# A graph kernel whose adjacency is loaded by quarters of columns and turned by VectorE instead of TensorE

## The chip, the cores and the metric

The kernel runs on one core of one Trainium2 chip. The metric is the time on the device of one execution in microseconds; where there are several runs, their median is given.

## What is computed

Two graph layers over 4096 nodes with 256 features, each behind a layer norm and a ReLU, each added to its input:

```python
# layer 1
mask = (adj > 0)                                  # adj: 4096 x 4096 int32
agg  = mask @ h / max(rowsum(mask), 1)
out  = relu(concat(h @ W_self + b_self, agg @ W_nb + b_nb) @ W_comb + b_comb)
# layer 2, 4 heads of 64
Wh = h @ W ; sl, sr = Wh . a_l, Wh . a_r
e  = leaky_relu(sl[i] + sr[j]) where adj[i, j] + (i == j) > 0, else -inf
out = elu(softmax(e) @ Wh)
# both:  x = x + layer(relu(layernorm(x)))
```

The adjacency is 64 MB of int32, and is read once.

## The kernel before

The program is written out for each engine by hand, with semaphores between them; what stands in an engine's block is the order in which it works, and `Fori` loops run the steady parts.

**First phase (to about 76 us).** `x` comes in 16 pairs of rows (256 nodes each) by SP's queue. They are normed and multiplied with the folded weights; the result is `g`, 16-bit high and low parts of the neighbour product for all 4096 nodes, and `own`, the node's own part, stored to HBM by GpSimd's queue.

**First layer (32 tiles of 128 nodes).** For a tile t, SP's queue loads its rows of the adjacency in two halves of 2048 columns into `stage` (`adj_rows`, L319), each as soon as the half before it in the same buffer is unpacked. VectorE turns int32 into bytes of 0 or 0xB8, the fp8 code of a number (`to_bits`, L946). ScalarE sums the bytes into the degree (L718). TensorE takes two bytes as one bf16 and transposes 16 blocks of 128x128 (`words`, L553); VectorE copies them from PSUM to `mT` (`copy_words`, L957), and GpSimd keeps a second copy in `mask` for layer 2 (`keep`, L433). TensorE then sums `g` over the neighbours: 32 products, each with weights of fp8 bytes read from `mT` at a step of two bytes (`sums`, L567). `post` (L969 to L994) makes x1 of the tile from the sum, the degree and the rows that GpSimd's queue brings back (L441), and its norm's numbers; ScalarE writes the normed h1 (L728). TensorE turns h1 (L577) and multiplies it with W (L586). These two stand in the middle and at the end of the next tile's sums. `set_self_edges` (L1008) sets the diagonal in `mask`, once for two tiles.

**Second layer (from about 379 us).** For each of 4 heads and 4 strips of 1024 nodes: ScalarE and VectorE write signs as bytes (L778, L1044), VectorE combines them with `mask` (L1054, L1065), and TensorE sums values over bytes of both results (`branch`, L630), 8192 products of 130 columns. These too read fp8 weights at a step of two bytes.

Of the kernel before, what the change touches and what calls it, by code (L numbers as in the profile page):

```python
# [23 lines left out]
F32 = mybir.dt.float32  # L24
F16 = mybir.dt.float16
BF16 = mybir.dt.bfloat16
# [29 lines left out]
VBLK = 2 * DV  # L56
CH = 4
NCH = NK // CH
NQ = NK // 2
ZR = 8  # L60
PR = 4


def build(nc, x, adj, W_self, b_self, W_nb, b_nb, W_comb, b_comb, W, a_l, a_r, out):
# [8 lines left out]
    out_v = out.rearrange("(s k p e) (h d) -> s h e p k d", s=NS, p=P, e=2, h=H)  # L73
    x_v = x.rearrange("(k p e) d -> k p (e d)", p=P, e=2)
    adj_v = adj.rearrange("(k p e) m -> k p (e m)", p=P, e=2)
    HALF = N // 2
    HK = NK // 2
    NP2 = NK // 2
    E1 = D + 3 * H
    WS = STRIP // 2  # L80
    with ExitStack() as ctx:
# [15 lines left out]
        mask32 = mask[:, :, :].bitcast(I32)  # L97
        sr = sb("sr", [P, NT, 3 * H], F32)
        diag = sb("diag", [P, 2 * P], U16)
# [3 lines left out]
        identb = sb("identb", [P, P], BF16)  # L103
# [11 lines left out]
        diagf = early(5, 2 * D, 2 * P).rearrange("p (e n) -> p e n", e=2)  # L115
        bcol = early(5, 2 * D + 2 * P, 4)
# [9 lines left out]
        shift = early(13, 64, 2)  # L126

# [3 lines left out]
        degp = sb("degp", [P, NT, 2], F32)  # L131
        mT = sb("mT", [P, 2, N // 2], BF16)
# [3 lines left out]
        deg = sb("deg", [P, 3], F32)  # L136
# [10 lines left out]
        shift1 = sb("shift1", [P, 1], F32)  # L147
# [22 lines left out]
        pos = mT[:, :, :].rearrange("p e m -> p (e m)").bitcast(I32).rearrange("p (k n) -> p k n", k=PR)  # L170
# [13 lines left out]
        ps_t = [t.bitcast(BF16) for t in ps_t32]  # L184
# [32 lines left out]
        stage_in = [sem(f"stage_in{i}") for i in range(2)]  # L217
# [3 lines left out]
        words_ready = sem("words_ready")  # L221
        words_copied = sem("words_copied")
        kept = sem("kept")
# [7 lines left out]
        norm1_ready = sem("norm1_ready")  # L231
# [65 lines left out]
        def _(sp):  # L297
# [25 lines left out]
            adj_rows(0, 0)  # L323
# [6 lines left out]
            adj_rows(0, 1)  # L330
            with sp.Fori(1, NK) as k:
                for e in range(2):
                    adj_rows(k, e)
# [7 lines left out]
            sp.wait_ge(words_ready, NT * 2)  # L341
            sp.wait_ge(deg_ready, NT * 2)
# [28 lines left out]
            def store(gr):  # L371
                sp.wait_ge(y_ready, gr + 1)
                for e in range(2):
                    sp.dma_start(out_v[gr % NS, gr // NS, e],
                                 y[:, :, :].rearrange("p (k e) d -> p e k d", e=2)[:, e]).then_inc(stored, 16)

            def next_s(gr):

                sp.wait_ge(act_signs, gr * ASIGN)
                sp.wait_ge(dve_signs, gr * DSIGN)  # L380
                load_s(gr + 1)
# [18 lines left out]
            sp.wait_ge(stored, 32 * NG)  # L400

        @block.gpsimd
        def _(pool):
            nc.gpsimd.memset(ident[:, :], 0.0).then_inc(zeroed, 1)
            nc.gpsimd.memset(diagf, 0.0).then_inc(zeroed, 1)
            nc.gpsimd.memset(ones[:, :], 1.0)
            nc.gpsimd.memset(eps[:, :], EPS).then_inc(consts, 1)
            pool.wait_ge(zeroed, 2)
            nc.gpsimd.affine_select(out=ident[:, :], in_=ident[:, :], compare_op=ALU.not_equal, fill=1.0,
                                    base=0, pattern=[[-1, P]], channel_multiplier=1).then_inc(consts, 1)  # L410
            for e in range(2):
                nc.gpsimd.affine_select(out=diagf[:, e, :], in_=diagf[:, e, :], compare_op=ALU.not_equal,
                                        fill=float(ONE << (8 * e)), base=0, pattern=[[-1, P]],
                                        channel_multiplier=1).then_inc(consts, 1)
# [67 lines left out]
        def _(pe):  # L482
# [74 lines left out]
            def sums(t, e, f):  # L557
# [11 lines left out]
                if f == 1:  # L569
                    last.then_inc(agg_ready, 1)  # L570
# [720 lines left out]
```

## Time and profile before

| | us |
|---|---|
| median of 3 runs (889.4 to 891.55) | 890.43 |
| the profiled execution | 888.39 |
| its span, first to last instruction | 886.8 |

| engine | busy us | share of the span |
|---|---|---|
| TensorE, products | 824.4 | 93% |
| TensorE, weight loads (beside the products) | 659.3 | 74% |
| VectorE | 719.6 | 81% |
| ScalarE | 696.3 | 79% |
| GpSimd | 153.4 | 17% |

The share is an average over three stages. The DMA engines, whose mean share is given beside the engines, moved 115 MB, 67 MB of it adjacency, nearly all of it in the first layer. A row by form gives a line of the program, the engine, what it writes and reads, how often, and the mean time of one in ns.

### The profile page before, as it was taken

To read this page: it belongs to the slowest core of one execution; us is meant where nothing else is said; L and a number is where in the kernel's file an instruction comes from. 1 tells how busy PE (TensorE), PEld (TensorE's weight loads), DVE (VectorE), ACT (ScalarE), POOL (GpSimd) and SP (SyncE) were. 2 spreads that over 40 slices of the span, in tenths; PEclk is the share of its full clock that TensorE was granted. 3 is DMA by queue.
4 is the path that set the end of the run, shared out by engine and by line. 5 is a ranking of instruction groups with operands and counts; after the bars stand their busy time and mean duration, and the time that the engine had idled before them with its cause. 6 is when DMAs were issued, how large, how long until landed. Compare 5 with 4: busy or idle time off the path is not lost.

```text
span 886.8 us, 26720 instructions
## 1 busy us (share of the span) xinstructions
PE 824.4 (93%) x10276; PEld 659.3 (74%) x10276; DVE 719.6 (81%) x1373; ACT 696.3 (79%) x989; POOL 153.4 (17%) x221
## 2 busy tenths in 40 slices
PE   3998899999999999869899989999899999899996
PEld 3343355555555555449899989999899999899996
DVE  3897677787778777578879898888998889989885
ACT  2675556666666666488989999999998999989993
POOL 0111345454646463300000000000000000000000
PEclk9999899999999999969999999999999999999998
DMA  6345767878787878540041011121101410111011
GB/s 219 111 150 210 281 243 281 306 278 312 279 312 273 313 277 308 91 111 23 2 95 48 0 48 48 37 58 48 48 14 33 95 47 6 42 48 47 0 24 35
DMA packets 74875, 115.32 MB, mean 130 GB/s; under 512 B 55553, under 2 KB 57473, under 8 KB 66657
## 3 DMA queue, kind: packets, MB, share of 16 engines
q1 hardware_dynamic: 67472, 94.19, 32.2%
q0 software_dynamic: 7376, 20.85, 7.4%
q8 instruction: 8, 0.13, 0.1%
q14 instruction: 19, 0.15, 0.1%
HBM read 98.17 MB, written 16.85 MB: 130 GB/s over the span
## 4 chain that ended last, share of the span: by engine, by line
PE 66%; DVE 16%; ACT 7%; issue 5%; DMA 4%; DVEq 1%; SPq 1%; ACTq 0%
PE ps_a L567 12%; PE ps_t L630 12%; PE ps_x L630 12%; PE ps_a L630 11%; PE ps_h L630 6%; PE ps_w L630 6%; DMA stage<-in_adj 3%; ACT stage L778 3%; DVE bits L946 3%; DVE stage L1054 2%; PE ps_x L525 1%; PE ps_t L553 1%; PE ps_w L586 1%; PE ps_a L525 1%; ACT late L728 1%
## 5 line engine op out<-in xcount | busy, mean ns | idle before, releaser
L567 PE MATMUL ps_a<-g,mT 128*128 128x512 f16 x1024 | 234.8, 383 | 2.5 <-DVE mT L957 2.5
L778 ACT ACTIVATE stage<-bits,sr 128x1024 int8<-128x1024 f32 x192 | 203.6, 1167 | 1.1 <-PE ps_w L630 1.1
L778 ACT ACTIVATE stage<-rows,sr 128x1024 int8<-128x1024 f32 x192 | 203.1, 1172 | 1.1 <-PE ps_w L630 1.1
L1054 DVE SCALAR_TENSOR_TENSOR stage<-stage,mask 128x1024 int32<-128x1024 int32 x128 | 156.4, 1222 | 42.1 <-ACT stage L778 41.6
L567 PEld LDWEIGHTS ps_a<-g,mT 128*128 128x128 fp8e4 x1024 | 100.9, 99 | 112.7 <-issue 7.4
L718 ACT ACTIVATE junk<-bits 128x2048 uint8<-128x2048 uint8 x64 | 122.2, 1910 | 70.4 <-DVE bits L946 65.7
L1065 DVE TENSOR_SCALAR mT<-stage 128x1024 int32<-128x1024 int32 x128 | 88.0, 687 | 13.4 <-PE ps_w L630 13.4
L630 PE MATMUL ps_x<-g,stage 128*128 128x130 f16 x1024 | 79.9, 220 | 13.8 <-DVE late L1097 10.4
L946 DVE TENSOR_SCALAR bits<-stage 128x2048 uint8<-128x2048 int32 x64 | 78.5, 1264 | 13.3 <-DMA stage<-in_adj 13.3
L630 PE MATMUL ps_x<-g,mT 128*128 128x130 f16 x1024 | 79.6, 220 | 2.3 <-DVE mT L1065 2.3
L630 PE MATMUL ps_t<-g,stage 128*128 128x130 f16 x1024 | 81.0, 220 | 0.1
L630 PE MATMUL ps_a<-g,stage 128*128 128x130 f16 x1024 | 80.5, 221 | 0.0
L630 PE MATMUL ps_t<-g,mT 128*128 128x130 f16 x1024 | 79.4, 220 | 0.0
L630 PE MATMUL ps_a<-g,mT 128*128 128x130 f16 x1024 | 78.7, 219 | 0.0
L630 PEld LDWEIGHTS ps_x<-g,stage 128*128 128x128 fp8e4 x1024 | 63.9, 97 | 14.9 <-issue 14.8
L630 PEld LDWEIGHTS ps_x<-g,mT 128*128 128x128 fp8e4 x1024 | 63.9, 97 | 2.9 <-issue 2.9
L630 PEld LDWEIGHTS ps_t<-g,stage 128*128 128x128 fp8e4 x1024 | 64.6, 97 | 0.8
L630 PEld LDWEIGHTS ps_a<-g,stage 128*128 128x128 fp8e4 x1024 | 64.4, 98 | 0.0
L630 PEld LDWEIGHTS ps_t<-g,mT 128*128 128x128 fp8e4 x1024 | 63.9, 97 | 0.0
L630 PEld LDWEIGHTS ps_a<-g,mT 128*128 128x128 fp8e4 x1024 | 63.2, 97 | 0.0
L957 DVE COPY mT<-ps_t 128x1024 bf16<-128x1024 bf16 x64 | 41.3, 686 | 15.8 <-PE ps_t L553 15.2
L630 PE MATMUL ps_h<-g,stage 128*128 128x130 f16 x512 | 50.5, 221 | 0.0
(136 smaller groups left out, 1289.4 us busy)
## 6 DMA issues: line engine op xcount, KB each, us to landing
stage<-in_adj SPq DMA_DIRECT2D x64, 1024.0 KB, 6.9
mask<-in_x SPq DMA_DIRECT2D x16, 256.0 KB, 2.8
own_scratch<-mask POOLq DMA_DIRECT2D x16, 256.0 KB, 3.0
rows<-in_x POOLq DMA_DIRECT2D x32, 128.0 KB, 3.0
rows<-own_scratch POOLq DMA_DIRECT2D x32, 128.0 KB, 5.4
x_scratch<-late POOLq DMA_DIRECT2D x32, 128.0 KB, 2.1
bits<-s_scratch SPq DMA_DIRECT2D x8, 512.0 KB, 4.4
rows<-s_scratch SPq DMA_DIRECT2D x8, 512.0 KB, 4.7
```

The lines of the kernel that those rows point to most:

```text
L525: last = nc.tensor.matmul(ps_mm[2 * b + e][:, :], hT[hp][:, b, (2 * e + c) * P:(2 * e + c + 1) * P], ab[wp][:, c, :], start=(c == 0 and hp ...
L553: last = nc.tensor.transpose(ps_t[f][:, q * P:(q + 1) * P], w[:, q * P:(q + 1) * P], identb[:, :])
L567: last = nc.tensor.matmul(ps_a[e][:, :], m[:, kk, b, :], g[:, 2 * kk + b, :], start=(kk == 0 and b == 0), stop=(kk == NK - 1 and b == 1))
L586: last = nc.tensor.matmul(ps_w[:, 0:E1], h1T[:, e, hp, c * P:(c + 1) * P], wext[:, wp, c, :], start=(c == 0 and hp + wp == 0), stop=(c == ...
L630: last = nc.tensor.matmul(acc[j][:, br * VBLK:(br + 1) * VBLK], bytes_of(ring[:, k % size, j * (P // 2):(j + 1) * (P // 2)])[:, b, :], val ...
L718: nc.scalar.activation(junk[:, :], bits[:, f, :], ACT.Copy, accum_out=degp[:, bass.ds(t, 1), f:f + 1].rearrange("p o f -> p (o f)")).then_ ...
L728: nc.scalar.activation(h1[:, e, :], x1[:, e, :], ACT.Relu, bias=shift1[:, 0:1], scale=rstd1[:, 0:1]).then_inc(h1_ready, 1)
L778: nc.scalar.activation(sign_bytes(sgn, k, b), srow[gr % 2], ACT.Sign, bias=sr[:, 2 * k + b, H + gr // NS:H + gr // NS + 1]).then_inc(act_s ...
L946: nc.vector.tensor_scalar(bits[:, f, :], stage[:, f, :], 0.0, float(ONE), ALU.is_gt, ALU.mult).then_inc(bits_ready, 1)
L957: nc.vector.tensor_copy(mT[:, e, f * HK * P:(f + 1) * HK * P], ps_t[f][:, :]).then_inc(words_copied, 1)
L1054: nc.vector.scalar_tensor_tensor(sg, sg, SIGN_BITS, mask32[:, 2 * q:2 * q + 2, gr % NS * WS:(gr % NS + 1) * WS], ALU.bitwise_xor, ALU.bitw ...
L1065: nc.vector.tensor_scalar(pos[:, 2 * q % PR:2 * q % PR + 2, :], sgn[:, 2 * q % ZR:2 * q % ZR + 2, :].bitcast(I32), 1, TWO_BITS, ALU.logica ...
```

## The change

The change rewrites how the mask of the first layer comes into being, and with it how nodes are laid over partitions and tiles.

- **Nodes.** A partition p now holds nodes 32p to 32p + 31, and tile t is the nodes with 32p + t. `x`, `out` and the scratch rows are viewed so.
- **Load.** A half of a tile is now two transfers of 512 KB. Each brings 32 rows; partition group a (of four) gets columns 1024a to 1024a + 1023 of these rows. The HBM pattern is 4 quarters, 32 rows (512 KB apart), 1024 columns (4 KB). There are three buffers of a half, `stage` and the new `stage2`, instead of two.
- **Turn.** VectorE's 32x32 transpose works on words of four bytes, reading `bits` at a step of eight words, and writes the tile's 8 x 128 words straight into `mask`. TensorE's `words`, VectorE's `copy_words` and GpSimd's `keep` are gone. `mask` now holds four bytes of neighbours per word, and TensorE reads its fp8 weights at a step of four bytes, in both layers. The tiles' mask is made three tiles ahead.
- **Degrees.** A row's columns now lie in four partition groups, so ScalarE sums each of four units apart (1024 bytes each), and a small product (`degree_sums`) and four small steps (`degrees`) add them up for two tiles at a time.
- **Norm.** h1 is written by VectorE without the ReLU, which moves to the two copies that follow the turn of h1. A bits step stands between the norm's halves in `post`, where VectorE waited for ScalarE.
- **Self edges** are set at each tile. The loops of the first layer are written out. The output of a strip is one transfer instead of two.

```diff
-    adj_v = adj.rearrange("(k p e) m -> k p (e m)", p=P, e=2)
+    adj_v = adj.rearrange("(u j t) (a n) -> t u a j n", u=UN, t=NT, a=UN)
...
-            def adj_rows(k, e):
-                for f in range(2):
-                    if not (isinstance(k, int) and k == 0 and e == 0):
-
-                        sp.wait_ge(bits_ready, (k * 2 + e) * 2 - 1 + f)
-                    sp.dma_start(stage[:, f, :],
-                                 adj_v[bass.ds(k, 1), :, e * N + f * HALF:e * N + (f + 1) * HALF]
-                                 .rearrange("o p m -> p (o m)")).then_inc(stage_in[f], 16)
+            def adj_rows(n):
+                t, f = n // 2, n % 2
+                if n >= 3:
+                    sp.wait_ge(bits_ready, n - 2)
+                for u in range(2):
+                    sp.dma_start(halves[n % 3][:, u * STRIP:(u + 1) * STRIP], adj_v[t, 2 * f + u]
+                                 ).then_inc(stage_in[n % 3], 16)
...
-            def words(t, e):
-
-                for f in range(2):
-                    pe.wait_ge(bits_ready, t * 2 + (f + 1))
-                    if not isinstance(t, int) or t >= 1:
-                        pe.wait_ge(words_copied, t * 2 + (f - 1))
-                    w = bits[:, f, :].bitcast(BF16)
-                    for q in range(HK):
-                        last = nc.tensor.transpose(ps_t[f][:, q * P:(q + 1) * P], w[:, q * P:(q + 1) * P],
-                                                   identb[:, :])
-                    last.then_inc(words_ready, 1)
...
+                for i in range(first, end):
+                    last = nc.tensor.matmul(ps_a[e][:, :],
+                                            bytes_of(mask32[:, i // QUAD, t * P:(t + 1) * P])[:, i % QUAD, :],
+                                            g[:, i, :], start=i == 0, stop=i == NT - 1)
...
+            def turn(t):
+
+                dve.wait_ge(bits_ready, 2 * t + 2)
+                nc.vector.transpose(mask32[:, :, t * P:(t + 1) * P],
+                                    bits[:, :, :].rearrange("p f m -> p (f m)").bitcast(I32)
+                                    .rearrange("p (n c) -> p c n", c=NC)).then_inc(turned, 1)
...
+            for t in range(NT - 2):
+                more = t + 3 < NT
+                post(t, lambda: to_bits(t + 3, 0) if more else None)
+                if more:
+                    to_bits(t + 3, 1)
+                low_h1T(t, t % 2)
+                if more:
+                    turn(t + 3)
+                set_self_edges(t)
+                if t % 2 == 1:
+                    degrees((t + 1) // 2)
```

On SP's queue, at the end of the first phase and the start of the first layer, before (`stage` takes the adjacency, `mask` here holds the first phase's buffers):

```order
L319 DMA stage<-in_adj 128x2048 x2
L324 UNCONDITIONAL_BRANCH
L324 ISA
L328 ISA
L328 DMA mask<-in_x 128x512
L328 ISA
L328 DMA mask<-in_x 128x512
L324 REGISTER_ALU
L324 COMPARE_AND_BRANCH
L319 DMA stage<-in_adj 128x2048 x2
```

and now:

```order
L322 DMA stage<-in_adj 128x1x1024 x4
L327 UNCONDITIONAL_BRANCH
L327 ISA
L331 ISA
L331 DMA mask<-in_x 128x512
L331 ISA
L331 DMA mask<-in_x 128x512
L327 REGISTER_ALU
L327 COMPARE_AND_BRANCH
L322 DMA stage<-in_adj 128x1x1024 x124
```

The first two halves are issued ahead of the x loads of the loop in both; they are now four transfers instead of two, and all others follow the loop.

On TensorE, one tile of the first layer before (`ps_a` the neighbour sum, `ps_t` the transposed bytes, `ps_h` h1 turned, `ps_w` its product):

```order
L567 MATMUL ps_a<-g,mT 128x512 x16
L553 MATMUL ps_t<-identb,bits 128x128 x16
L577 MATMUL ps_h<-ident,late 128x128 x2
L567 MATMUL ps_a<-g,mT 128x512 x16
L586 MATMUL ps_w<-late 128x268 x6
```

and two tiles now:

```order
L527 MATMUL ps_a<-g,mask 128x512 x21
L548 MATMUL ps_h<-ident,late 128x128 x2
L539 MATMUL ps_t<-junk 128x8
L527 MATMUL ps_a<-g,mask 128x512 x11
L557 MATMUL ps_w<-late 128x268 x6
L527 MATMUL ps_a<-g,mask 128x512 x21
L548 MATMUL ps_h<-ident,late 128x128 x2
L527 MATMUL ps_a<-g,mask 128x512 x11
L557 MATMUL ps_w<-late 128x268 x6
```

The 16 transposes are gone, one product of 8 columns for the degrees stands in every other tile, and h1 is turned after 21 of the 32 products instead of 16.

On VectorE, a tile of the first layer now (the copies from `ps_t` to `mT`, the small steps on `deg` and the step on `shift` stood here before):

```order
L943 SCALAR_TENSOR_TENSOR late<-ps_a,dinv,rows 128x256
L945 SCALAR_TENSOR_TENSOR late<-ps_a,dinv,late 128x256
L947 SCALAR_TENSOR_TENSOR late<-late,rows 128x256
L950 BN_STATS stats<-late 128x6
L954 BN_AGGR mv<-stats 128x2
L903 TENSOR_SCALAR bits<-stage 128x2048
L957 RECIPROCAL rstd<-std 128x1
L958 TENSOR_SCALAR late<-late,mv,rstd 128x256
L903 TENSOR_SCALAR bits<-stage 128x2048
L964 SCALAR_TENSOR_TENSOR late<-ps_h,late 128x256
L909 STREAM_TRANSPOSE mask<-bits 128x8x128
L971 SCALAR_TENSOR_TENSOR mask<-diag,mask 128x128
```

The first of the two bits steps now stands inside `post`, and the turn and the self edges end the tile.

## Rows read from the trace of the kernel before

**Rows 1.** Busy us of each engine by stretch, TensorE's clock, DMA share.

```profile
core 0: us, PE busy (x) PEld busy (x) DVE busy (x) ACT busy (x) POOL busy (x), PEclk, DMA share, GB/s
150.00:200.00 50.00, 49.46 (x309) 26.87 (x308) 40.30 (x89) 32.88 (x53) 27.25 (x36) 1.00 0.79 288
...
98.90:374.90 276.00, 265.92 (x1665) 145.18 (x1666) 210.95 (x468) 174.62 (x301) 134.74 (x179) 0.99 0.77 275
212.00:229.80 17.80, 17.62 (x113) 9.70 (x112) 13.97 (x32) 11.75 (x20) 9.19 (x12) 1.00 0.78 297
...
375.00:400.00 25.00, 16.65 (x151) 12.63 (x149) 19.68 (x46) 20.32 (x33) 2.31 (x5) 0.73 0.42 104
450.00:600.00 150.00, 147.00 (x2576) 146.42 (x2574) 132.38 (x207) 141.85 (x174) 0.00 (x0) 1.00 0.21 49
```

**Rows 2.** The chain that ended last: start us, us, what.

```profile
75.83 2.36 DVE bits L946 x2
...
344.30 0.91 PE ps_t L553 x16
...
348.93 12.39 DMA stage<-in_adj
361.35 0.06 DVE bits L946
...
375.23 3.47 PE ps_a L567 x16
```

**Rows 3.** The page's head and its part 2.

```profile
span 886.8 us, 26720 instructions
...
PEclk9999899999999999969999999999999999999998
```

**Rows 4.** DMA, 150 to 200 us, 40 slices: share, GB/s; issues.

```profile
DMA  6099999438999982989997378999837799983299
GB/s 223 13 243 406 364 370 426 170 105 216 393 354 308 429 328 69 210 334 410 308 416 308 111 177 328 393 315 423 344 118 174 285 393 364 423 354 105 79 302 419
...
q1 hardware_dynamic: 1580, 11.50, 61.6%
q0 software_dynamic: 1056, 2.88, 17.2%
...
stage<-in_adj SPq DMA_DIRECT2D x12, 1024.0 KB, 6.1
x_scratch<-late POOLq DMA_DIRECT2D x6, 128.0 KB, 2.1
rows<-in_x POOLq DMA_DIRECT2D x6, 128.0 KB, 3.1
rows<-own_scratch POOLq DMA_DIRECT2D x6, 128.0 KB, 5.5
wh_scratch<-late POOLq DMA_DIRECT2D x6, 128.0 KB, 6.3
```

**Rows 5.** Timeline, 200 to 212 us: start, duration, engine, line.

```profile
201.60 1.06 PE L553 MATMUL ps_t<-identb,bits 128*128 128x128 bf16 x16
...
211.05 1.29 DVE L957 COPY mT<-ps_t 128x1024 bf16<-128x1024 bf16 x2 [0.19 <-PE ps_t L553]
```

**Rows 6.** VectorE's groups by form, 100 to 350 us, then 450 to 850: count, busy, mean ns.

```profile
L946 DVE TENSOR_SCALAR bits<-stage 128x2048 uint8<-128x2048 int32 x56 | 68.7, 1268 | 0.0
L957 DVE COPY mT<-ps_t 128x1024 bf16<-128x1024 bf16 x56 | 36.1, 686 | 15.3 <-PE ps_t L553 15.2
...
L987 DVE BATCH_NORM_STATS2 stats<-late 128x6 f32<-128x256 f32 x27 | 11.5, 428 | 0.9
...
L1008 DVE TENSOR_TENSOR mask<-mask,diag 128x128 int32 x14 | 9.5, 675 | 0.0
...
L971 DVE RECIPROCAL deg<-deg 128x1 f32<-128x1 f32 x28 | 4.6, 164 | 1.0
L994 DVE SCALAR_TENSOR_TENSOR shift<-mv,rstd 128x1 f32<-128x1 f32 x28 | 4.5, 160 | 1.0
L970 DVE TENSOR_SCALAR deg<-deg 128x1 f32<-128x1 f32 x28 | 4.3, 154 | 1.0
L969 DVE TENSOR_REDUCE deg<-degp 128x1 f32 x27 | 3.7, 139 | 0.0
...
L1054 DVE SCALAR_TENSOR_TENSOR stage<-stage,mask 128x1024 int32<-128x1024 int32 x106 | 129.5, 1222 | 32.5 <-ACT stage L778 32.0
L1065 DVE TENSOR_SCALAR mT<-stage 128x1024 int32<-128x1024 int32 x106 | 72.9, 687 | 10.3 <-PE ps_w L630 10.3
...
L1044 DVE TENSOR_SCALAR stage<-bits,sr 128x1024 uint8<-128x1024 f32 x55 | 41.3, 751 | 0.0
```

**Rows 7.** ScalarE's groups by form, 212 to 229.8 us, then its signs, 450 to 850.

```profile
L718 ACT ACTIVATE junk<-bits 128x2048 uint8<-128x2048 uint8 x4 | 7.6, 1910 | 4.1 <-DVE bits L946 3.7 <-ACT junk L718 0.4
L728 ACT ACTIVATE late<-late,shift,rstd 128x256 f32<-128x256 f32 x2 | 1.2, 600 | 0.9 <-DVE shift L994 0.9
...
L718 ACT ACTIVATION_READ_ACCUMULATOR junk<-bits x4 | 0.7, 186 | 0.0
...
L778 ACT ACTIVATE stage<-bits,sr 128x1024 int8<-128x1024 f32 x166 | 175.8, 1172 | 0.6 <-PE ps_w L630 0.6
```

**Rows 8.** TensorE's weight loads, 100 to 350 us, then 450 to 850.

```profile
L567 PEld LDWEIGHTS ps_a<-g,mT 128*128 128x128 fp8e4 x884 | 87.0, 98 | 93.9 <-issue 2.5
L553 PEld LDWEIGHTS ps_t<-identb,bits 128*128 128x128 bf16 x432 | 26.4, 98 | 6.4
L586 PEld LDWEIGHTS ps_w<-late 128*128 128x128 f16 x168 | 16.4, 98 | 8.5
...
L630 PEld LDWEIGHTS ps_t<-g,stage 128*128 128x128 fp8e4 x853 | 53.2, 97 | 0.7
```

**Rows 9.** Timeline of the start: SP's queue, then VectorE.

```profile
5.96 0.74 SPq L311 DMA_DIRECT2D mask<-in_L_gnn_a_r  x1
6.74 0.92 SPq L319 DMA_DIRECT2D stage<-in_adj  x2
8.43 26.99 SPq L328 DMA_DIRECT2D mask<-in_x  x5
...
24.57 0.75 DVE L858 BATCH_NORM_STATS2 mask<-mask 128x6 f32<-128x256 f32 x2
```

More of the change, by code:

```diff
@@ L56 @@
 VBLK = 2 * DV
+TURN = 21
 CH = 4
@@ L329, in _ @@
                                  ).then_inc(x_in[b], 16)
[L330 to L333, printed above, removed]
+            for n in range(2, 2 * NT):
+                adj_rows(n)
             sp.wait_ge(sr_ready, NJ)
@@ L589, in wh_product @@
                 last.then_inc(wh_mm_ready, 1)
-            def tile(t, e, first=False, final=False):
-                sums(t, e, 0)
-                if not final:
-                    words(t + 1, 1 - e)
-                if not first:
-                    turn_h1(t - 1, 1 - e)
-                sums(t, e, 1)
-                if not first:
-                    wh_product(t - 1, 1 - e)
-            pe.wait_ge(consts, 6)
-            words(0, 0)
-            pe.wait_ge(mm_free, 2 * NK + 4)
-            tile(0, 0, first=True)
-            tile(1, 1)
-            with pe.Fori(1, NK - 1) as k:
-                for e in range(2):
-                    tile(k * 2 + e, e)
-            tile(NT - 2, 0)
-            tile(NT - 1, 1, final=True)
+            pe.wait_ge(mm_free, 2 * NK + 4)
+            pe.wait_ge(const_step, 3)
+            degree_sums(0)
+            for t in range(NT):
+                sums(t, 0, TURN)
+                if t:
+                    turn_h1(t - 1, 1 - t % 2)
+                if t % 2 == 0 and t:
+                    degree_sums(t // 2)
+                sums(t, TURN, NT)
+                if t:
+                    wh_product(t - 1, 1 - t % 2)
             turn_h1(NT - 1, 1)
@@ L937, in _ @@
                 two_pairs(i)
-            def to_bits(t):
-                for f in range(2):
-                    dve.wait_ge(stage_in[f], (t + 1) * 16)
-                    if not (isinstance(t, int) and t == 0):
-                        dve.wait_ge(words_ready, t * 2 + (f - 1))
-                        dve.wait_ge(deg_ready, t * 2 + (f - 1))
-                    nc.vector.tensor_scalar(bits[:, f, :], stage[:, f, :], 0.0, float(ONE), ALU.is_gt, ALU.mult
-                                            ).then_inc(bits_ready, 1)
@@ L963, in link, with post @@
+            def post(t, between):
+                STEPS = 4
+                e, k = t % 2, t // 2
                 def link(ins, n):
@@ L1031, in signs @@
+            degrees(0)
+            for t in range(NT - 2):
+                more = t + 3 < NT
+                post(t, lambda: to_bits(t + 3, 0) if more else None)
+                if more:
+                    to_bits(t + 3, 1)
+                low_h1T(t, t % 2)
+                if more:
+                    turn(t + 3)
+                set_self_edges(t)
+                if t % 2 == 1:
+                    degrees((t + 1) // 2)
             def signs(gr, q):
@@ L1248, in hold, with dve_has, bytes_of, sign_bytes @@
     eng.sem_inc(waits_passed, 1)
-def dve_has(k, b):
-    return b == 1 and k % 2 == 1
-ASIGN = sum(not dve_has(k, b) for k in range(NK) for b in range(2))
-DSIGN = NT - ASIGN
-def sign_bytes(sgn, k, b):
-    return sgn[:, k % ZR, :].rearrange("p (n b) -> p b n", b=2)[:, b, :]
+def dve_has(b):
+    return b == QUAD - 1
+DSIGN = sum(dve_has(b) for b in range(QUAD))
+def bytes_of(t):
+    return t.bitcast(F8).rearrange("p (n b) -> p b n", b=QUAD)
+def sign_bytes(sgn, q, b):
+    return sgn[:, q % ZR, :].rearrange("p (n b) -> p b n", b=QUAD)[:, b, :]
 def fac_col(fac, i, gr, j):
```

359 lines of the change are left out of this document (159 added, 200 removed).

## The prediction

> **What bounds the kernel now.** Read the busy time by stage first [rows 1]. The first layer's 32 tiles fill most of the stretch from 98.9 to 374.9 us, the second layer 375 to the end. In the first, TensorE is busy 265.92 of 276.00 us, VectorE 210.95, ScalarE 174.62, and the DMA engines 0.77. Two tiles last 17.8 us (the same line of the program starts at 212.00 and at 229.80): 8.9 us a tile, and TensorE is busy 17.62 of those 17.8. So TensorE sets the pace of this layer, VectorE has 1.9 us of slack in a tile (13.97 us in two), and the transfers, at 297 GB/s, stand close behind: a tile's 2.1 MB of adjacency and 0.5 MB of rows take 0.78 of it.
>
> Second, the chain that ended last [rows 2]. At the end of the layer the last piece of adjacency lands at 361.3 us, and the last sum ends at 378.7: 17.4 us later, which is the work of the last tiles. From there to the end of the span (886.8 us, [rows 3]) are 508 us of second layer. It is bound by TensorE (147.00 of 150 us), and the change touches it only in how bytes lie.
>
> Third, the DMA view of 150 to 200 us [rows 4]: no transfer of adjacency stands alone; the sixteen engines are busy 0.79 of the time and move 288 GB/s [rows 1, 4], so a busy engine moves 288/0.79/16 = 22.8 GB/s; the best slice, 429 GB/s, is 26.8 for each.
>
> The profiled execution took 888.4 us, 1.6 above its span, and 2.0 below the median of 890.4.
>
> **The change part by part.**
>
> *TensorE.* The 16 transposes of a tile go; they end a tile's work 0.91 to 1.06 us later than without [rows 2, 5]. Sums, h1 transposes and Wh product stay: 8.9 - 0.9 = 8.0 us of TensorE a tile. One 8-column product for two tiles is new, under 0.1 us.
>
> *VectorE.* Out: two copies of 0.686 us, the shift (0.16), and every tile's three small degree steps (0.46), for which four stand in two tiles (0.3 a tile). In: the norm of 128x256 (0.43, as the row of the same size), a self-edge step for each tile instead of two (0.675 a step, so 0.34 more), and the 32x32 turn of 128x1024 words. No row shows a turn. Its bounds: 0.69 us, the copy of as many elements, and 5.4, if each element cost what one of the 128 in the self-edge step costs (675 ns) [rows 6]. I take 1.2, as the two-source operation on 1024 words (1222 ns) shows one element a cycle [rows 6]. Sum: 7.0 - 1.4 - 0.15 - 0.16 + 0.43 + 0.34 + 1.2 = 7.3 us. That fits under 8.0; at a turn of 1.9 us it would tie. ScalarE: four pieces of 1024 (about 1.17 + 0.19 each) for two of 1.91 + 0.19 is 1.2 more, the norm 0.6 less, on 5.9 now: 6.5 us, under 8.0 [rows 1, 7]. GpSimd loses its copies. All of this is hidden under TensorE's 8.0 and alone would give 31 x 0.9 = 28 us.
>
> *Weights read with a step of four bytes, not two.* Loading fp8 at step two takes 97 or 98 ns, 16-bit weights at step one 98 [rows 8]: the step doesn't show. I take nothing, in both layers. The upper bound is a load that no longer hides behind a 130-column product: 2576 products in 150 us are 58 ns each [rows 1], so each ns would be 8 us.
>
> *The load.* This decides. Before, a transfer is 128 rows of 8 KB, partition outermost on both sides. Now the HBM side reads a, j, n: its outermost dimension is the four column quarters, and 32 rows lie inside it (`adj_v`; 4 KB pieces). If a transfer is dealt out to engines by its outermost dimension, as it is written, no more than four engines can have a share, where 128 gave all sixteen one. Every transfer in the trace has 128 outermost, so no row shows either a limit or its absence; the shape is all there is. The price is bounded from rows. If all sixteen still work: 2.6 MB a tile at 22.8 x 16 GB/s is 7.2 us, under TensorE's 8.0, nothing. If four: a half (1 MB) is 262 KB for each of the four, and the rows and stores of GpSimd's queue add 16 KB (a sixteenth of 256 KB for half a tile, its four transfers of 128 KB a tile [rows 4]), 279 KB in all. At 26.8 GB/s that is 10.4 us, at 22.8 it is 12.2. I take 25.5, 10.9 us, nearer the best slice, as four engines crowd nothing else. That is 21.8 us a tile against 8.0, and nothing hides it.
> The Trainium skill, "DMA: Bandwidth & Descriptors", section "Why a DMA increments its semaphore by 16 and not by 1", says that the number of engines is the largest number up to 16 that divides the count of the slowest dimension on both sides, which for 4 and 128 is 4, always the lowest-numbered ones. By that rule both transfers of a half share the same four engines; no run here shows it yet. Its section on rules adds that an outermost dimension below 16 confines a transfer to so many engines.
>
> *With four engines, what waits.* SP's queue: the new order puts the x loads of the first phase behind two halves (2 MB) [rows 9]. Four engines need 524 KB/25.5 = 20.6 us for them, from about 12 us when the weights are in, so the third x pair lands near 32 us; VectorE takes it up at 24.6 today [rows 9]. The first phase ends 8 us later: 75.8 [rows 2] becomes 84. The third half lands before. From then 61 halves follow each other: the third buffer keeps two queued while one is unpacked, and VectorE's 7.3 us and TensorE's 8.0 (16 at half clock) in 21.8 leave no gap. Last landing: 84 + 1.5 (bits) + 61 x 10.9 + 2 = 752. The tail stays 17.4, the second layer 508: span 1278, plus 1.6 outside and 2.0 to the median: 1281 us.
>
> TensorE will idle most of each tile. Where it idled before, from 375 to 400 us, the granted clock fell to 0.73 [rows 1]; a tile's 8.0 us at 2.4 GHz are up to 16 at 1.2 GHz, still under 21.8, so that costs nothing but 0 to 3 us in the tail.
>
> **The rivals.**
>
> *A. Sixteen engines carry the load, faster.* The sum is then TensorE's: 890.4 - 28 = 862 us (855 to 880; the start may gain a little by the third buffer, and VectorE at 7.3 with a chain of short steps may lose some). For it: nothing in the trace says that a transfer is ever carried by fewer. Against it: the shape.
>
> *B. Sixteen engines, and the turn is slow; VectorE becomes the bound.* It decides from a turn of 1.9 us (less gain) and turns the sign at 2.8, where VectorE needs 8.9. The input is read with a step of eight words. At the far bound of 5.4 us a tile takes 11.5: 890 + 31 x 2.6 = 971; at two cycles an element (2.3) it is 8.4, which gives 875. Against it: the sign step, whose bytes are written at step two, takes 751 ns for 1024 against 687 for the plain one [rows 6], so a step between elements costs little there.
>
> *C. Four engines but dearer pieces:* the rows of a piece lie 512 KB apart in HBM instead of 32; at 12.2 us a half the result is 1281 + 61 x 1.3 = 1360. This is in the forecast's own range.
>
> **How the numbers follow.** Forecast (four engines, with C) 0.83; A 0.12; B 0.05, of which 0.02 slower, 0.02 faster, 0.01 the same. The range goes from 26.8 GB/s (10.4 us: 1250), less for a first phase that isn't delayed (8) and a shorter tail, to 12.2 us (1360): 1235 to 1365, holding nearly all of the forecast's 0.83. About 0.2% is what a measurement of this kernel can tell from no change. Faster: 0.12 + 0.02 = 0.14; same 0.01; slower 0.85.
>
> **What would show it.** In the page of the changed kernel: the DMA share near 0.25 to 0.3 throughout the first layer with about 100 to 120 GB/s, a tile of 21 to 24 us, VectorE's bits step waiting for the adjacency, a half-clock TensorE, and a second layer of unchanged 508 us. The turn's row shows 1.2 us or not; the weight loads show 97 ns or not. I am wrong on the whole if the adjacency's transfers land in 6 to 7 us as today; then the tile is 8.0 us and the rows of TensorE and VectorE tell A from B.

## The result

| | us |
|---|---|
| changed kernel, median of 4 runs (1377.3 to 1380.57) | 1378.82 |
| kernel before, beside it, median of 4 runs (888.53 to 891.55) | 889.91 |
| ratio | 1.550, 95% interval 1.545 to 1.555 |
| profiled execution of the changed kernel, its span | 1377.71, 1376.2 |

The change makes the kernel 489 us slower, 98 more than the 391 forecast. The head of the page of the changed kernel, with its 40 slices of 34 us (DMA in tenths, then GB/s) and the chain that ended last:

```profile
span 1376.2 us, 24635 instructions
...
PEclk9986677767677777777677789999999999999999
DMA  4342323233332323232332230211121112111101
GB/s 141 123 146 111 121 112 123 114 124 116 121 124 113 124 113 124 114 124 114 124 124 113 74 75 16 61 31 30 31 61 31 31 31 61 30 31 31 30 15 23
...
ACT 34%; DMA 30%; SPq 21%; PE 8%; DVE 4%; issue 2%; DVEq 0%; ACTq 0%
ACT stage L728 30%; DMA stage<-in_adj 28%; SPq L322 21%; ACT late L751 2%; DVE bits L903 2%; DMA mask<-in_x 1%; PE ps_x L589 1%; PE ps_t L589 1%; PE ps_a L589 1%; ACT g L739 1%; PE ps_a L527 1%; PE ps_x L499 1%; PE ps_a L499 1%; DVE mask L828 1%; PE ps_h L589 1%
```

Two things stand there. The first layer is a transfer: the adjacency and SP's queue (`SPq L322`, which issues it) hold 49% of the chain. The second is new and was not forecast: ScalarE's signs, `L728`, hold 30%, where TensorE bound this layer before.

The same kernel's busy time by stretch: the first layer, the second layer, and 200 us in the middle of the second (columns as in [rows 1]):

```profile
98.30:776.20 677.90, 347.63 (x1216) 146.95 (x1216) 225.48 (x409) 171.14 (x385) 65.20 (x119) 0.72 0.31 117
795.60:1376.20 580.60, 500.13 (x8218) 491.18 (x8216) 449.76 (x697) 561.40 (x575) 2.64 (x5) 0.94 0.15 37
1000.00:1200.00 200.00, 179.92 (x2985) 178.05 (x2982) 156.49 (x239) 200.00 (x202) 0.00 (x0) 0.95 0.18 42
```

Against [rows 1], the first layer's DMA share has fallen from 0.77 to 0.31 and its GB/s from 275 to 117, while the time rose from 276 to 678 us. In the second layer ScalarE, the fourth pair of columns, is busy 200.00 of 200 us, TensorE 0.90 of them; before it was TensorE with 0.98. Counted from the end of the last sum, as the prediction counts it, that layer lasts 579 us (797.3 to 1376.2) for 508. The end of the last sum in TensorE's timeline (start, duration):

```profile
794.78 2.54 PE L527 MATMUL ps_a<-g,mask 128*128 128x512 f16 x11
```

Bits steps and turns in two halves of one tile, in the changed kernel's timeline of VectorE (start, duration, idle time before and what ended it):

```profile
395.53 1.23 DVE L903 TENSOR_SCALAR bits<-stage 128x2048 uint8<-128x2048 int32 x1 [10.11 <-DMA stage<-in_adj]
396.68 0.42 DVE L964 SCALAR_TENSOR_TENSOR late<-ps_h,late 128x256 f16<-128x256 f32 x1
397.01 2.02 DVE L909 STREAM_TRANSPOSE mask<-bits 128x1024 int32<-128x1024 int32 x1
...
405.67 1.23 DVE L903 TENSOR_SCALAR bits<-stage 128x2048 uint8<-128x2048 int32 x1 [3.32 <-DMA stage<-in_adj]
...
417.50 1.23 DVE L903 TENSOR_SCALAR bits<-stage 128x2048 uint8<-128x2048 int32 x1 [10.09 <-DMA stage<-in_adj]
```

A tile takes 22.0 us here (395.53 to 417.50), before it was 8.9 [rows 1], and the adjacency releases 62 of the 64 bits steps. All the rest of VectorE's tile fits in the gaps.

The groups by form of the changed kernel that answer to [rows 6] to [rows 8] (count, busy, mean ns, idle time before and its releaser; where operations of one group overlap, busy counts the overlap once):

```profile
L728 ACT ACTIVATE stage<-bits,sr 128x1024 int8<-128x1024 f32 x192 | 258.2, 1601 | 0.0
L728 ACT ACTIVATE stage<-rows,sr 128x1024 int8<-128x1024 f32 x192 | 256.6, 1609 | 0.0
...
L676 ACT ACTIVATE junk<-bits 128x1024 uint8<-128x1024 uint8 x128 | 134.9, 1054 | 439.5 <-DVE bits L903 439.2
...
L1019 DVE SCALAR_TENSOR_TENSOR stage<-stage,mask 128x1024 int32<-128x1024 int32 x128 | 156.8, 1225 | 113.7 <-ACT stage L728 113.7
...
L903 DVE TENSOR_SCALAR bits<-stage 128x2048 uint8<-128x2048 int32 x64 | 78.5, 1227 | 442.9 <-DMA stage<-in_adj 442.9
L909 DVE STREAM_TRANSPOSE mask<-bits 128x1024 int32<-128x1024 int32 x32 | 64.6, 2019 | 0.1
L1010 DVE TENSOR_SCALAR stage<-bits,sr 128x1024 uint8<-128x1024 f32 x64 | 53.2, 833 | 0.0
...
L589 PEld LDWEIGHTS ps_t<-g,stage 128*128 128x128 fp8e4 x2048 | 132.8, 100 | 0.2
```

The sign step in ScalarE takes 1601 to 1609 ns; it was 1172 [rows 7]. Its size and types are the same; `sign_bytes` gives it every fourth byte to write instead of every second. Successive steps overlap, so what a step costs ScalarE is its busy time over its count: 258.2 us/192 = 1.34 us, and 203.6/192 = 1.06 before. The same step in VectorE went from 751 [rows 6] to 833. The weight loads, which also read every fourth byte, are at 100 ns for 97 [rows 8].

### The profile page after: what moved, and what is told of

Its sections match the earlier page's. It is cut to its first block, busy times and chain, and to the rows that moved or that the text cites. A ratio compares the mean times of both kernels' runs of the same rounds, so it can differ in the third digit from the quotient of the medians.

```text
span 1376.2 us, 24635 instructions
## 1 busy us (share of the span) xinstructions
PE 926.9 (67%) x9796; PEld 677.5 (49%) x9796; DVE 749.4 (54%) x1329; ACT 789.0 (57%) x1085; POOL 80.6 (6%) x152
## 4 chain that ended last, share of the span: by engine, by line
ACT 34%; DMA 30%; SPq 21%; PE 8%; DVE 4%; issue 2%; DVEq 0%; ACTq 0%
ACT stage L728 30%; DMA stage<-in_adj 28%; SPq L322 21%; ACT late L751 2%; DVE bits L903 2%; DMA mask<-in_x 1%; PE ps_x L589 1%; PE ps_t L589 1%; PE ps_a L589 1%; ACT g L739 1%; PE ps_a L527 1%; PE ps_x L499 1%; PE ps_a L499 1%; DVE mask L828 1%; PE ps_h L589 1%
## 5 line engine op out<-in xcount | busy, mean ns | idle before, releaser
L676 ACT ACTIVATE junk<-bits 128x1024 uint8<-128x1024 uint8 x128 | 134.9, 1054 | 439.5 <-DVE bits L903 439.2
L527 PE MATMUL ps_a<-g,mask 128*128 128x512 f16 x1024 | 312.5, 474 | 0.0
L728 ACT ACTIVATE stage<-bits,sr 128x1024 int8<-128x1024 f32 x192 | 258.2, 1601 | 0.0
L728 ACT ACTIVATE stage<-rows,sr 128x1024 int8<-128x1024 f32 x192 | 256.6, 1609 | 0.0
L1019 DVE SCALAR_TENSOR_TENSOR stage<-stage,mask 128x1024 int32<-128x1024 int32 x128 | 156.8, 1225 | 113.7 <-ACT stage L728 113.7
L589 PE MATMUL ps_x<-g,stage 128*128 128x130 f16 x2048 | 165.0, 225 | 66.8 <-DVE late L1058 51.6
L527 PEld LDWEIGHTS ps_a<-g,mask 128*128 128x128 fp8e4 x1024 | 123.1, 121 | 167.3 <-issue 99.8
L589 PE MATMUL ps_t<-g,stage 128*128 128x130 f16 x2048 | 164.3, 224 | 0.0
L589 PE MATMUL ps_a<-g,stage 128*128 128x130 f16 x2048 | 163.9, 224 | 0.0
L589 PE MATMUL ps_w<-g,stage 128*128 128x130 f16 x1024 | 102.1, 223 | 0.0
L1027 DVE TENSOR_SCALAR stage<-stage 128x1024 int32<-128x1024 int32 x128 | 88.0, 687 | 3.2 <-PE ps_w L589 3.1
L589 PEld LDWEIGHTS ps_h<-g,stage 128*128 128x128 fp8e4 x1024 | 71.0, 100 | 0.0
L589 PEld LDWEIGHTS ps_w<-g,stage 128*128 128x128 fp8e4 x1024 | 70.7, 99 | 0.1
```

The lines of the kernel that those rows point to most:

```text
L527: last = nc.tensor.matmul(ps_a[e][:, :], bytes_of(mask32[:, i // QUAD, t * P:(t + 1) * P])[:, i % QUAD, :], g[:, i, :], start=i == 0, stop ...
L589: last = nc.tensor.matmul(acc[j][:, br * VBLK:(br + 1) * VBLK], bytes_of(ring[:, q % size, j * P:(j + 1) * P])[:, b, :], val[:, QUAD * q + ...
L676: nc.scalar.activation(junk[:, 0:STRIP], bits[:, u // 2, u % 2 * STRIP:(u % 2 + 1) * STRIP], ACT.Copy, accum_out=degp[:, t, u:u + 1]).then ...
L728: nc.scalar.activation(sign_bytes(sgn, q, b), srow[gr % 2], ACT.Sign, bias=sr[:, QUAD * q + b, H + gr // NS:H + gr // NS + 1]).then_inc(ac ...
L1019: nc.vector.scalar_tensor_tensor(sg, sg, SIGN_BITS, mask32[:, q, gr % NS * STRIP:(gr % NS + 1) * STRIP], ALU.bitwise_xor, ALU.bitwise_and) ...
L1027: nc.vector.tensor_scalar(pos[:, q % PR, :], sgn[:, q % ZR, :].bitcast(I32), 1, TWO_BITS, ALU.logical_shift_right, ALU.bitwise_and).then_i ...
```

## The experiments

They ran in three groups, each on a chip of its own with the kernel before beside it. The first group (891.4 us for the kernel before) is four outermost, eight outermost, all sixteen engines, and the sign bytes of the changed kernel. The second (890.9) is the order of the transfers, GpSimd's queue, sign bytes of the kernel before at step four, and more signs in VectorE. The third (889.5) is step one, the weights, the straight turn, and both gains together.

### Four outermost, alone

> The kernel before with one thing added: each adjacency transfer is written as 4 x 32 rows, with 4 outermost (the rows of a tile come in another order, so the mask belongs to permuted nodes; nothing else differs; pieces stay 8 KB, rows 32 KB apart at most). Theory: four engines, a half of 1 MB every 10.9 to 11.3 us, 31 x (22.5 - 8.9) = 420 us more, 1290 to 1320 us; DMA share near 0.3. Rival (piece size or row distance did it): 890 us.

```diff
-    adj_v = adj.rearrange("(k p e) m -> k p (e m)", p=P, e=2)
+    adj_v = adj.rearrange("(k j a e) m -> k a j (e m)", a=4, j=P // 4, e=2)
```

Measured: 1310.91 us, ratio 1.473 (1.462 to 1.484). Its DMA view of 200 to 600 us, the queue of the adjacency:

```profile
DMA packets 8456, 48.56 MB, mean 121 GB/s; under 512 B 1340, under 2 KB 1340, under 8 KB 3717
...
q1 hardware_dynamic: 4887, 38.82, 23.8%
```

Same bytes, same 8 KB pieces, TensorE's transposes all in place, and only the order of the dimensions changed: the first layer becomes that of the changed kernel. 23.8% of sixteen is 3.8 engines, and 38.82 MB in 400 us through them is 25.5 GB/s for each. Four outermost in HBM is the cause, and it accounts by itself for the whole of the first layer's loss: the last bits step stands at 778.3 us here, at 777.4 in the changed kernel. The edit also moves the rows inside a group from 32 KB to 128 KB apart (the 32 KB in the expectation is the distance between groups). That isn't what holds four engines: with 512 KB between rows sixteen engines work, two sections on.

### Eight outermost, alone

> As the run with 4 outermost, but 8 x 16 rows, 8 outermost. Theory (engines = outermost count): half the time for a half, 5.6 us, a tile of 11.3 us, 31 x 2.4 = 74 us more: 955 to 970 us. Rival (the four engines are a special case of this layout and not a matter of the count): 890 us or 1300 us.

The edit is the one above with `a=8, j=P // 8`. Measured: 1095.23 us, ratio 1.230 (1.217 to 1.244), 125 us above the upper end expected. DMA view, 150 to 350 us:

```profile
DMA packets 6019, 33.98 MB, mean 170 GB/s; under 512 B 1040, under 2 KB 1040, under 8 KB 2704
...
q1 hardware_dynamic: 3521, 27.14, 44.9%
```

44.9% of sixteen is 7.2 engines: the count came as expected. Each moves 27.14 MB/200 us/7.2 = 18.9 GB/s, a quarter less than when four work. The rate of one engine isn't a constant that the count can be multiplied with. The rows of a group lie 256 KB apart here, and whether the count or this distance lowers the rate no run isolates.

### All sixteen engines in the changed layout

> The changed kernel with one thing undone: a half of a tile is four transfers, one for each quarter of the columns, each with 32 rows outermost on the HBM side and 32 partitions on the other (before: two transfers with the four quarters outermost). Layout, bytes and piece size (4 KB) stay. Theory (a transfer gets as many engines as its outermost count allows): adjacency at 280 GB/s or more, a tile of 8.0 to 8.4 us set by TensorE and VectorE (its turn measured 2.02 us), the first layer ends near 350 us, the second stays at 580 us: 930 to 940 us. Rival (pieces of 4 KB with rows 512 KB apart are slow in themselves): the tile stays at 20 us or more, 1300 us and above.

```diff
-    adj_v = adj.rearrange("(u j t) (a n) -> t u a j n", u=UN, t=NT, a=UN)
+    adj_v = adj.rearrange("(w u j t) (a n) -> t w a j u n", w=2, u=2, t=NT, a=UN)
...
-                for u in range(2):
-                    sp.dma_start(halves[n % 3][:, u * STRIP:(u + 1) * STRIP], adj_v[t, 2 * f + u]
-                                 ).then_inc(stage_in[n % 3], 16)
+                for a in range(UN):
+                    sp.dma_start(halves[n % 3][32 * a:32 * (a + 1), :].rearrange("p (u n) -> p u n", u=2),
+                                 adj_v[t, f, a]).then_inc(stage_in[n % 3], 16)
```

Measured: 987.41 us, ratio 1.110 (1.102 to 1.118), some 50 us more than expected. DMA, 150 to 350 us:

```profile
DMA packets 16838, 53.22 MB, mean 266 GB/s; under 512 B 3876, under 2 KB 3876, under 8 KB 16824
...
q1 hardware_dynamic: 12984, 42.56, 83.9%
```

The first layer comes back almost whole: the last bits step stands at 386.1 us, where the changed kernel has it at 777.4 and the kernel before at 361.3. But the engines are now full (0.84 for this queue, 1.04 in all) and each moves 15.9 GB/s, against 22.8 in [rows 1, 4]. A tile lasts 10.0 us (the median distance between the bits steps of successive tiles), still longer than the 8.9 of before, and is bound by its transfer. That is what the expectation missed: it took the rate of the kernel before. The other 71 us of the loss are the second layer, which this edit doesn't touch.

### The order of the four transfers

> The run with a transfer for each quarter (32 partitions, sixteen engines; 987 us, 262 GB/s, a tile of 9.7 us), with the quarters issued in the order 0, 2, 1, 3. If its transfers are held up because sixteen engines write the same 32 partitions, and the two halves of the partitions have ways in of their own, neighbours in the queue now go to different halves and overlap: 280 GB/s or more, 950 to 975 us. If it is the size and distance of the pieces, nothing changes: 987 us within 5.

```diff
-                for a in range(UN):
+                for a in (0, 2, 1, 3):
```

Measured: 975.22 us, ratio 1.096 (1.089 to 1.102), 12 us under the kernel above, which ran on another chip. Time and rate (279 GB/s from 150 to 350 us) lie at the edge of what its theory expected. It has the last bits step at 374.2, and on the same chip a kernel with the order 0 to 3 (the balanced one, below) has it at 383.9. On a third chip the two orders stand at 353.9 and 394.4 (the last two experiments). The order 0, 2, 1, 3 is ahead in both pairs. How much it is worth stays open: each time is that of one execution, and four executions of the kernel with 353.9 lie 24 us apart. Nor is it shown that the two halves of the partitions have ways in of their own.

### The same four-outermost transfers on GpSimd's queue

> The changed kernel's transfers of the adjacency as they are (four quarters outermost), but issued by GpSimd's queue between its rows and stores, not by SP's. If a transfer of four shares uses the same four engines whoever issues it: 1379 us again. If this queue gives successive transfers different engines, four transfers in flight use all sixteen: DMA share 0.7 to 0.9, 280 GB/s or more, a tile of 8.0 to 8.6 us, first layer done near 355 us, second layer still 580: 930 to 950 us. A risk is that GpSimd issues each of them slowly, or that they stand behind its waits for ScalarE.

```diff
-                    sp.dma_start(halves[n % 3][:, u * STRIP:(u + 1) * STRIP], adj_v[t, 2 * f + u]
+                    pool.dma_start(halves[n % 3][:, u * STRIP:(u + 1) * STRIP], adj_v[t, 2 * f + u]
```

The calls were moved with it: halves 0 and 1 ahead of the first phase's stores, the others between the row loads and stores of the first layer. Measured: 1088.70 us, ratio 1.223 (1.216 to 1.230), well above what was expected. DMA, 200 to 300 us:

```profile
DMA packets 18706, 20.30 MB, mean 203 GB/s; under 512 B 13774, under 2 KB 13774, under 8 KB 18701
...
q0 software_dynamic: 17661, 20.23, 105.5%
```

The stream of the same transfers isn't confined to four engines when another queue issues it: all sixteen are full. Whether each takes four others in turn or is spread wider, the shares don't tell. They move only 203 GB/s, and three packets in four are under 512 bytes. The small packets aren't what slows it: the 12734 of 4 bytes in this queue took 0.10 of the sixteen engines' time, at 12 ns each, while its 4927 packets of 4 KB took 0.96, at 311 ns each. In the changed kernel, from 200 to 300 us, a packet of 4 KB of the adjacency takes 166 ns. Why it takes nearly twice as long from this queue stays open.

### The sign bytes of the changed kernel at step two

> The changed kernel with the sign bytes of the second layer written at a step of two bytes again (two blocks of 2048 bytes instead of one of 4096), everything else as changed, weights still read at step four; the second layer's numbers are then not those of the reference. Theory (ScalarE's writes at step four cost the second layer its 73 us): ScalarE's sign step is back from 1605 to about 1167 ns, the second layer from 581 to about 508 us, 1300 to 1310 us in all. Rival (weights read at step four take it, or hold up ScalarE's writes): sign step above 1400 ns, 1360 us or more.

```diff
-    return sgn[:, q % ZR, :].rearrange("p (n b) -> p b n", b=QUAD)[:, b, :]
+    return sgn[:, q % ZR, b // 2 * 2 * STRIP:(b // 2 + 1) * 2 * STRIP].rearrange("p (n b) -> p b n", b=2)[:, b % 2, :]
```

Measured: 1310.16 us, ratio 1.472 (1.461 to 1.482): 69 us less than the changed kernel. ScalarE's groups and the second layer's window:

```profile
L728 ACT ACTIVATE stage<-bits,sr 128x1024 int8<-128x1024 f32 x192 | 203.9, 1167 | 1.1 <-PE ps_w L589 1.0
L728 ACT ACTIVATE stage<-rows,sr 128x1024 int8<-128x1024 f32 x192 | 203.4, 1168 | 2.5 <-PE ps_w L589 2.4
```
```profile
795.60:1309.00 513.40, 482.79 (x8226) 476.74 (x8223) 440.03 (x697) 466.23 (x576) 2.54 (x5) 0.97 0.17 42
```

TensorE still reads all weights at a step of four here, and from the end of the last sum (798.7 us) the layer takes 510 us, for 579 in the changed kernel and 508 before. So of the 71 us that the second layer lost, 68 are the writes, and ScalarE waits for TensorE again (`<-PE ps_w`).

### The sign bytes of the kernel before at step four, and at step one

> The kernel before with the sign bytes of the second layer written at a step of four bytes, into a block of 4096, by both engines; everything else, weights at step two among it, stays (the bytes then don't match the mask's order, so the second layer's numbers are not the reference's). Theory (the write step alone slows ScalarE): the sign step goes from 1167 to about 1600 ns, the second layer from 508 to 570 to 580 us, 955 to 965 us in all. Rival (it takes the step-four write and the step-four weight reads together): sign step at most 1300 ns, under 910 us.

```diff
-    return sgn[:, k % ZR, :].rearrange("p (n b) -> p b n", b=2)[:, b, :]
+    slot = k % ZR // 2 * 2
+    return (sgn[:, slot:slot + 2, :].rearrange("p k n -> p (k n)")
+            .rearrange("p (n b) -> p b n", b=4)[:, 2 * (k % 2) + b, :])
```

Measured: 954.26 us, ratio 1.072 (1.066 to 1.078). The loss alone, put into the kernel before, is 63 us in all. From the end of the last sum (373.4 us) the second layer takes 576 us, 68 more than before; the first layer of the profiled execution ended 5 us earlier than that of the kernel before.

```profile
L778 ACT ACTIVATE stage<-bits,sr 128x1024 int8<-128x1024 f32 x192 | 254.6, 1506 | 0.0
L778 ACT ACTIVATE stage<-rows,sr 128x1024 int8<-128x1024 f32 x192 | 252.9, 1498 | 0.0
```

> The kernel before, with ScalarE's and VectorE's sign bytes of the second layer written side by side (step one) where they are written at step two; TensorE and the product still read them at step two, so the output mixes columns and only its time is used. Theory (the price is of the write alone and grows with its step): 1167 ns at step two and about 1500 at step four leave at step one something near the plain 128x1024 pass of the changed kernel's degree piece, 1054 ns; VectorE's step falls from 751 to about 687. TensorE bounds the second layer, so the whole stays within 3 us of 890. Rival (steps one and two cost alike, and the price begins above two bytes): 1167 ns stays. Either way the time is the same; the row decides.

```diff
-    return sgn[:, k % ZR, :].rearrange("p (n b) -> p b n", b=2)[:, b, :]
+    return sgn[:, k % ZR, b * STRIP:(b + 1) * STRIP]
```

Measured: 889.51 us, ratio 1.000 (0.997 to 1.004).

```profile
L778 ACT ACTIVATE stage<-bits,sr 128x1024 int8<-128x1024 f32 x192 | 203.6, 1163 | 1.0 <-PE ps_w L630 1.0
...
L1044 DVE TENSOR_SCALAR stage<-rows,sr 128x1024 uint8<-128x1024 f32 x64 | 47.8, 747 | 0.0
```

Here the expectation fell and its rival held. Step one costs what step two costs, on both engines: 1163 and 1167 ns, 747 and 751. Step four, in the same kernel, costs about 1500 and 825 to 827. The price isn't proportional to the step; it begins above two bytes.

### The weights of the kernel before read at step four

> The kernel before, with TensorE's fp8 weights of the second layer read at a step of four bytes (the signs still written at two, so the output is of other columns and only the time is used). Theory (the reads are free, as the prediction took them, and only the write was missed): 888 to 893 us, weight loads of 97 to 100 ns. Rival (the reads cost too, and were hidden behind the slower ScalarE in the changed kernel): each ns on a product is about 8 us, so 900 or more.

```diff
+                slot = 2 * q % size
+                pair = ring[:, slot:slot + 2, :].rearrange("p k n -> p (k n)")
+                words = pair[:, j * P:(j + 1) * P].bitcast(F8).rearrange("p (n b) -> p b n", b=4)
...
-                            bytes_of(ring[:, k % size, j * (P // 2):(j + 1) * (P // 2)])[:, b, :],
+                            words[:, 2 * (k % 2) + b, :],
```

Measured: 893.06 us, ratio 1.003 (0.999 to 1.007), the interval takes in no change. The loads in `branch` are at 98 to 99 ns, for 97 [rows 8]. The read is free, or costs a few us at most.

### The turn reading its words in order

> The kernel of e1_load16 (four transfers a half, one for each quarter), with the turn reading its 1024 words in order where it read them at a step of eight; the mask then holds words of other columns, so only the time is used. Theory (the turn's 2.02 us come from the step of its reads): it falls to about 1.2 us, one element a cycle, as the prediction took. Rival (a turn costs that by itself, two cycles a word): 2.0 us again. In both cases VectorE is not the bound there (37.5 of 50 us busy), so the time stays at e1's 982 to 992 us.

```diff
                                     bits[:, :, :].rearrange("p f m -> p (f m)").bitcast(I32)
-                                    .rearrange("p (n c) -> p c n", c=NC)).then_inc(turned, 1)
+                                    .rearrange("p (c n) -> p c n", c=NC)).then_inc(turned, 1)
```

Measured: 989.66 us, ratio 1.112 (1.103 to 1.122), the time of the sixteen-engine kernel.

```profile
L909 DVE STREAM_TRANSPOSE mask<-bits 128x1024 int32<-128x1024 int32 x32 | 39.5, 1233 | 0.1
```

1233 ns for the changed kernel's 2019: read in order, the turn takes as long as the two-source operation on as many words (1225 ns), as the prediction had it; the step of eight words costs the other 0.79 us. The bound it competes with is elsewhere, so the whole doesn't move.

### More signs in VectorE, and both gains together

> The run with a transfer for each quarter, and in the second layer VectorE takes 12 of 32 sign steps instead of 8 (a second one in every other group of four). ScalarE is busy all of the time there and VectorE 0.77. If ScalarE's sign steps are what bounds the second layer: ScalarE 3.7 us a group instead of 4.4, VectorE 3.9, the second layer 580 to about 515 us, 915 to 930 us in all. If the bound is another (bytes at step four slow whoever reads them), 970 us or more.

```diff
-def dve_has(b):
+def dve_has(q, b):
...
-    return b == QUAD - 1
+    return b == QUAD - 1 or (b == 1 and q % 2 == 1)
```

This is the sixteen-engine kernel with 12 of 32 sign steps in VectorE, where 8 were; the waits that count them go with it. Measured: 936.36 us, ratio 1.052 (1.047 to 1.057), a little over the range expected: from the end of the last sum the second layer takes 531 us, where 515 was expected. It is now shared out, with each of three engines busy 467.63 to 476.62 of the 510 us from 420 to 930:

```profile
420.00:930.00 510.00, 476.62 (x8145) 471.40 (x8142) 469.54 (x723) 467.63 (x488) 0.00 (x0) 0.98 0.16 38
```

> e8_signs_balanced with the order of the quarters of e7_quarters_0213: the best of the changed layout so far. If the two gains lie in different layers they add: 936.4 less 12.2 is 924 us (918 to 930), still slower than before by 3 to 4 per cent, all of it in the first layer's transfers and the second layer's writes. If they do not add, 936.

Measured: 904.02, 904.44, 916.07 and 927.83 us, median 910.25, ratio 1.023 (1.012 to 1.034), better than expected. The DMA view of 150 to 350 us, of this kernel and then of the one with the straight turn, which ran on the same chip in the order 0 to 3. The two differ in the turn and in who makes the signs too, but in the first layer the transfers bind both:

```profile
q1 hardware_dynamic: 15135, 48.39, 82.1%
```
```profile
q1 hardware_dynamic: 12496, 40.95, 85.0%
```

The order 0, 2, 1, 3 gives 18.4 GB/s for each busy engine, the other 15.1, and the last bits step stands at 353.9 instead of 394.4. The expectation took 12 us for the order, from runs on two chips; between these two executions it is 40, of which some can be the spread named above. Of everything tried in the changed layout this is the best. Its first layer is 7 us ahead of the kernel before (353.9 against 361.3), and what follows its last bits step is 548.6 us for 525.5. The signs eat the gain three times over, and no version that beats the kernel before was found.

## Why the prediction was right, and where it fell short

The direction and the main cause were right; the time lies 14 us above the upper end of the range. From the span of 1278 forecast to 1376.2 measured:

| step | forecast | measured | us |
|---|---|---|---|
| first bits step | 84 | 87.5 | +3.5 |
| 61 halves | 10.9 each | 11.25 each, on average | +21.5 |
| from the last bits step to the end of the last sum | 17.4 | 19.9 | +2.5 |
| second layer, from there to the end | 508 | 578.9 | +70.9 |
| sum | | | +98.4 |

**The load: right, a little mis-sized.** Four engines carry it, as the expression for `adj_v` let one read. The experiment with four outermost in the kernel before shows this alone, at 25.5 GB/s for an engine, the value that the prediction took. In the steady part of the changed kernel a half takes 11.0 us (22.0 a tile) for the 10.9 forecast, and an engine moves 24.7 GB/s (37.98 MB from 200 to 600 us at a share of 24.0%). Its pieces are 4 KB instead of 8 and its rows further apart; Rival C named both, and put too much on them (12.2 us). With several transfers of the queue in flight the share stays at four engines, so they all use the same four. The Trainium skill, "DMA: Bandwidth & Descriptors", section "Why a DMA increments its semaphore by 16 and not by 1", says that the counts of the slowest dimensions of both sides set the number of engines; the shares of 24% and 45% at counts of 4 and 8 agree. It gives the count alone, and the 18.9 GB/s at eight show that the time needs the rate beside it. Which four these are no row here tells.

**"The third half lands before": wrong, some 6 us.** SP's queue issues it behind the x loads, at 79.1 us:

```profile
14.29 64.60 SPq L331 DMA_DIRECT2D mask<-in_x  x14
79.10 47.13 SPq L322 DMA_DIRECT2D stage<-in_adj  x12
```

VectorE took the third half at 94.9 us and the fourth at 108.0, where the sum has the fourth 14.4 us behind the first bits step, at 101.9. Another 7 of the 21.5 us stand at the end: two bits steps lie 17.7 us apart there (748.5 to 766.2). A transfer of 4 KB, `s_scratch<-sr`, is in flight beside the last halves and takes 33.3 us to land; no run shows whether it holds them up. What is left, 8 us over 58 halves, is the rate.

**The first phase: right, 3.5 us short.** SP's queue was the wait. The third pair of x lands late, in the chain of the changed kernel:

```profile
14.29 20.52 DMA mask<-in_x
34.91 0.76 DVE mask L808 x2
```

VectorE took it at 34.9 us; the prediction had it land near 32.

**"Weights read with a step of four bytes, not two": the step that failed.** It asked what the step costs the reader, TensorE, and answered rightly: nothing. It didn't ask what it costs the writers. The bytes that TensorE reads at a step of four are written at a step of four by ScalarE and VectorE, 384 and 128 times in the second layer. The prediction said of that layer that "the change touches it only in how bytes lie", and took nothing. ScalarE was busy 141.85 of 150 us there [rows 1], second to TensorE's 147.00. A busy time of 203.6 + 203.1 us for the signs becomes 258.2 + 256.6, 108 us more, on an engine with some 5% of slack; of these 108, 71 come through. This is the whole of the error outside the range: with 508 replaced by 578.9 the sum would have been 1352.

**VectorE: mis-sized and harmless.** The turn took 2.02 us, not 1.2. Its step of eight words was argued away with the sign step, "whose bytes are written at step two": but step two is just the case that costs nothing, so the row bore no witness on longer steps. In a tile of 22 us the 0.8 us are hidden.

**Rival A was mis-sized too.** It gave 7.2 us a tile to sixteen engines, at 22.8 GB/s each. With sixteen engines on groups of 32 partitions, the rate was 15.1 to 18.4, and the tile 8.8 to 10.3 us. Freeing TensorE of its transposes then brings 7 us at most of the 28 that rival A counted on, and with the signs it would have ended slower than before in any case.

**The clock.** The granted clock of 0.72 in the first layer, against 0.99, was foreseen and costs nothing there, since TensorE waits. In the tail it costs about 2 us, within the 0 to 3 of the prediction: 21 products of a sum take 6.28 us right behind the last bits step, at a granted clock of 0.66, and 4.53 us ten microseconds later, at 1.00. TensorE's weight loads in the changed kernel's first layer average 121 ns at the lower clock; at full clock, in the last experiment, the same loads take 100.

## What to carry to other kernels

Write out both sides of a transfer before its bytes are counted: on SP's queue what stood outermost decided how many engines carried it. Take the rate of one engine from a row of the same shape; it was 15.1 to 25.5 GB/s here. When a layout changes, price every access to the bytes that move, the writes as well as the reads and on each engine, and above all on the engine that is second in the busy table. A row at step two says nothing of step four: take a price from a row with the same step, or keep the whole range open.

## What the runs showed that was not expected

- A pass of 128x1024 from f32 to single bytes takes 1163 ns in ScalarE at step one, 1167 at two and 1472 to 1630 at four, by kernel; in VectorE 747, 751 and 825 to 839. Since steps overlap in ScalarE, its busy time a step rises by less, from 1.06 to 1.34 us.
- A transpose of 128x1024 words in blocks of 32x32 takes 1.23 us read in order, 2.02 to 2.04 at a step of eight words.
- A DMA engine moved 25.5 GB/s when four worked, 18.9 when eight did, and 15.1 to 18.4 when sixteen wrote 32 partitions at a time; but 22.8 when sixteen wrote 128 at a time [rows 1, 4], so the count alone doesn't set it. Two readings fit: that neighbouring engines or partitions share something on the way, or that the distance of the rows in HBM costs (32 KB at 22.8, 128 at 25.5, 256 at 18.9, 512 at 15.1 to 18.4, but 512 also at 24.7 with four engines). No run changes one of them alone.
- With four engines SP's issue of one transfer of the adjacency takes 4952 ns in the median, 333 in the kernel before. A queue without room for more fits this; no run tests it. Nothing else stood behind it on SP until the last half.
- Between the two orders of four transfers on one queue lie 10 us in one pair of executions and 40 in another.
- From GpSimd's queue a packet of 4 KB took 311 ns in an engine, for 166 from SP's with four engines and 255 with sixteen.
